# A routed expert stage with slots handed out in blocks of 64

## The reference

```python
# x: (2048, 512) after the layer norm; E = 8 experts, I = 352, top 2 of 8
logits = x @ router_w.T
probs = softmax(logits)
topk_w, topk_idx = top_k(probs, 2)
topk_w = topk_w / sum(topk_w)
for each expert e:
    acc += combine[:, e] * (silu(x @ gate_w[e]) * (x @ up_w[e]) @ down_w[e])
shared = silu(x @ s_gate_w + b) * (x @ s_up_w + b) @ s_down_w + b      # 704 wide
x = x + tanh(g_ffn[1]) * (acc + shared)
```

## Time and profile before

| | |
|---|---|
| time, median of 3 runs | 1132.05 us (1128.5 to 1133.57) |
| the profiled execution | 1127.45 us |
| its span, first to last instruction | 1125.4 us |
| busy share of the span: PE, DVE, ACT, POOL | 89%, 66%, 52%, 38% |
| granted TensorE clock over the span | 0.961 |
| stage of the tiles, PE | 845.4 us to about 1070 us, 39 tiles |

### The profile page before, as it was taken

One profiled execution on the slowest core, in us unless ns is written; L12 is line 12 of the kernel. 1 busy time (PEld: TensorE's weight loads), 2 busy tenths in 40 slices (PEclk: granted clock), 3 DMA queues, 4 the chain that ended last, 5 costly groups with the idle time before them and its releaser, 6 DMA issues. The chain is left out here.

```text
span 1125.4 us, 17282 instructions
## 1 busy us (share of the span) xinstructions
PE 1003.4 (89%) x5229; PEld 456.0 (41%) x5247; DVE 740.2 (66%) x1417; ACT 589.5 (52%) x888; POOL 430.1 (38%) x467
## 2 busy tenths in 40 slices
PE   0466879999779999999999995999999999899995
PEld 0243445555423223323332221454445555555542
DVE  6988988888788677487667858676244444433347
ACT  5897999999436677477557671524221111111110
POOL 1100435553501234133323533007508888790065
PEclk9988899999979999999999998989999999999998
DMA  8322940000532424314311032996525789865678
GB/s 322 126 75 75 303 193 1 1 1 1 130 81 75 130 63 91 96 59 82 96 35 59 22 85 82 234 358 224 220 83 115 207 209 202 198 166 128 157 286 293
DMA packets 196010, 150.88 MB, mean 134 GB/s; under 512 B 138420, under 2 KB 157492, under 8 KB 195432
## 3 DMA queue, kind: packets, MB, share of 16 engines
q1 hardware_dynamic: 187000, 121.02, 39.4%
q0 software_dynamic: 8080, 27.60, 7.3%
q10 hardware_dynamic: 864, 1.44, 0.5%
HBM read 73.03 MB, written 45.60 MB: 105 GB/s over the span
## 5 line engine op out<-in xcount | busy, mean ns | idle before, releaser
L1707 DVE CUSTOM_DVE_ANT_0 ajunk<-p_row,mask_row 128x512 bf16<-128x512 f32 x256 | 166.2, 686 | 61.1 <-PE p_row L1553 58.5
L1470 ACT ACTIVATE early_place<-p_col,mask_col,any_key 128x512 f32<-128x512 f32 x128 | 92.8, 776 | 63.2 <-PE p_col L1604 62.9
L1470 ACT ACTIVATE prob<-p_col,mask_col,any_key 128x512 f32<-128x512 f32 x128 | 93.3, 786 | 38.3 <-PE p_col L1604 37.8
L1360 POOL TENSOR_TENSOR o<-sum_a,rec 32x512 f32<-32x512 f32 x30 | 39.0, 1301 | 187.3 <-DMA rec<-inv_d 185.2
L1553 PE MATMUL p_row<-ks,early_place 99*128 99x512 f16 x256 | 100.6, 395 | 9.0 <-DVE top L1707 7.9
L1604 PE MATMUL p_col<-early_place,ks 101*128 101x512 f16 x256 | 97.7, 386 | 1.2 <-ACT early_place L1470 0.6
L2824 DVE SCALAR_TENSOR_TENSOR shid<-s_up,ssilu 128x352 f32<-128x352 f32 x39 | 20.4, 524 | 99.6 <-PE s_up L2743 99.5
L2756 PE MATMUL s_down<-mw,shT 128*128 (+1 forms) x351 | 82.1, 379 | 0.6 <-DMA shT<-shidr 0.6
L2681 ACT ACTIVATE ssilu<-s_gate 128x352 f32<-128x352 f32 x39 | 18.1, 463 | 118.4 <-PE s_gate L2743 118.4
L2743 PE MATMUL s_gate<-mw,spare 128*128 x444 | 73.8, 317 | 2.9 <-DMA spare<-x_slots 2.9
L2743 PE MATMUL s_up<-mw,spare 128*128 x444 | 72.3, 313 | 0.0
(11 more groups left out here) (380 smaller groups left out, 2132.1 us busy)
## 6 DMA issues: line engine op xcount, KB each, us to landing
x_slots<-nought SPq DMA_DIRECT2D x3, 3328.0 KB, 20.1
y_slots<-spare SPq DMA_DIRECT2D x39, 256.0 KB, 2.2
early_place<-in_ctx SPq DMA_DIRECT2D x8, 1024.0 KB, 6.2
early_place<-halves_d SPq DMA_DIRECT2D x45, 128.0 KB, 2.4
halves_d<-halves SPq DMA_DIRECT2D x18, 256.0 KB, 2.1
x<-in_x SPq DMA_DIRECT2D x4, 1024.0 KB, 7.4
w<-in_L_ffn_w SPq DMA_DIRECT2D x1, 4096.0 KB, 18.5
w<-in_L_ffn_w SPq DMA_DIRECT2D x4, 1024.0 KB, 4.7
```

The source lines that it names most:

```text
L1360: nc.gpsimd.tensor_tensor(o[q, :], (sum_a, sum_b)[g % 2][n % 2][q, :], rec[q, :], ALU.mult).then_inc(t_scaled, 1)
L1470: nc.scalar.activation(prob[s % 4][:, c, :], p_col[c][:], ACT.Exp, bias=mask_col[:, b, k:k + 1], scale=any_key[:, b:b + 1]).then_inc(t_exp, 1)
L1707: nc.vector.tensor_tensor_reduce(junk[:, n % 2, :], p_row[n % 2][:], mask_row[:, blk // HPG, :], 1.0, -3e38, ALU.add, ALU.max, top[blk % 2 ...
```

## The change

Slots are handed out in blocks of 64. TILES becomes 36 (the most that 4096 slots can need if each expert rounds up to 64, in pairs of blocks), of which FULL = 28 tiles hold one expert and the last eight hold two. The last block of expert j always lies in the second half of tile 28 + j. The remaining blocks of an expert are taken two at a time as whole tiles, in the order of the experts; single blocks left over, and whole tiles beyond 28, go to the first halves of the last eight tiles. `find_slots` and `find_owners` compute this, with more operations in the chain.

On PE the last eight tiles are written out (no loop), and each matmul in them becomes two: 64 columns of the stationary operand with the first expert's weights into partitions 0 to 63, and the other 64 columns with the second expert's weights into partitions 64 to 127. The second expert is a constant of the code, the first is read from `expert_of`. The tile count being even, the odd last tile of all engines' loops falls away, SP issues `late_T` before the last pair of tiles, and PE runs both halves of held chunk 0 between the last two down products.

```diff
-TILES = (B * S * CHOSEN + EXPERTS * (P - 1)) // P
+HALF = P // 2
+TILES = -(-((B * S * CHOSEN + EXPERTS * (HALF - 1)) // HALF) // 2)
+FULL = TILES - EXPERTS
...
-    tile_no = sb(st, "tile_no", [P, TILES, EXPERTS], F32)
+    half_no = sb(st, "half_no", [P, TILES, 2 * EXPERTS], BF16)
...
             def find_slots():
-                link(nc.vector.tensor_scalar(tiles[:], before[:, NT, :], 1.0 / P, (P - 1) / (2.0 * P), ALU.mult, ALU.add))
-                link(nc.vector.tensor_scalar(tiles[:], tiles[:], ROUND, None, ALU.add))
-                link(nc.vector.tensor_scalar(tiles[:], tiles[:], -ROUND, None, ALU.add))
-                link(nc.vector.tensor_copy(ends[:], tiles[:]))
+                link(nc.vector.tensor_scalar(singles, before[:, NT, :], 1.0 / HALF, (HALF - 1) / (2.0 * HALF), ALU.mult, ALU.add))
+                rounded(singles)
+                link(nc.vector.tensor_scalar(singles, singles, -1.0, 0.0, ALU.add, ALU.max))
+                link(nc.vector.tensor_scalar(pairs, singles, 0.5, -0.25, ALU.mult, ALU.add))
+                rounded(pairs)
+                link(nc.vector.scalar_tensor_tensor(singles, pairs, -2.0, singles, ALU.mult, ALU.add))
+                link(nc.vector.tensor_copy(ends[:], blocks[:]))
                 for e in range(1, EXPERTS):
-                    link(nc.vector.tensor_tensor(ends[:, e:e + 1], ends[:, e - 1:e], tiles[:, e:e + 1], ALU.add))
-                link(nc.vector.tensor_tensor(starts[:], ends[:], tiles[:], ALU.subtract))
-                link(nc.vector.tensor_scalar(starts[:], starts[:], float(P), None, ALU.mult))
-                link(nc.vector.tensor_tensor(before[:, 0:NT, :], before[:, 0:NT, :], starts[:].unsqueeze(1).broadcast_to([P, NT, EXPERTS]), ALU.add))
+                    link(nc.vector.tensor_tensor(ends[:, :, e:e + 1], ends[:, :, e - 1:e], blocks[:, :, e:e + 1], ALU.add))
+                link(nc.vector.tensor_tensor(starts[:], ends[:], blocks[:], ALU.subtract))
+                link(nc.vector.tensor_scalar(top, ends[:, 0, EXPERTS - 1:EXPERTS], 2.0, 2.0 * FULL, ALU.mult, ALU.max))
+                link(nc.vector.tensor_scalar(jump, pairs_end, float(FULL), None, ALU.max))
+                link(nc.vector.tensor_tensor(jump, jump, pairs_end, ALU.add))
+                link(nc.vector.tensor_tensor(jump, singles_start, jump, ALU.subtract))
+                link(nc.vector.tensor_scalar(jump, jump, top, float(P), ALU.add, ALU.mult))
+                link(nc.vector.tensor_scalar(lift, pairs_start, 2.0, -2.0 * FULL - 1, ALU.mult, ALU.add))
+                link(nc.vector.tensor_scalar(lift, lift, 0.0, float(HALF), ALU.max, ALU.mult))
+                link(nc.vector.tensor_tensor(back, number[:, 0, :], pairs_start, ALU.subtract))
+                link(nc.vector.tensor_scalar(back, back, FULL + 1.0, float(P), ALU.add, ALU.mult))
+                link(nc.vector.tensor_tensor(back, back, lift, ALU.subtract))
+                link(nc.vector.tensor_scalar(pairs, pairs, float(P), float(HALF), ALU.mult, ALU.add))
+                link(nc.vector.tensor_scalar(pairs_start, pairs_start, float(P), -float(HALF), ALU.mult, ALU.add))
+                link(nc.vector.scalar_tensor_tensor(own, count, float(HALF), each_token(back), ALU.is_lt, ALU.mult))
+                link(nc.vector.tensor_tensor(odd, count, each_token(pairs), ALU.is_ge))
+                link(nc.vector.tensor_tensor(odd, odd, each_token(jump), ALU.mult))
+                link(nc.vector.tensor_tensor(count, count, each_token(pairs_start), ALU.add))
+                link(nc.vector.tensor_scalar(shift, count, 1.0 / HALF, -(HALF - 1) / (2.0 * HALF), ALU.mult, ALU.add))
+                rounded(shift)
+                link(nc.vector.tensor_scalar(shift, shift, -2.0 * FULL, 0.0, ALU.add, ALU.max))
+                link(nc.vector.scalar_tensor_tensor(count, shift, float(HALF), count, ALU.mult, ALU.add))
+                link(nc.vector.tensor_tensor(count, count, odd, ALU.add))
+                link(nc.vector.tensor_tensor(count, count, own, ALU.add))
...
+            for n in range(2):
+                body(PAIRS_OF_TILES - 1, n, False)
...
+            def parts_of(r, n):
+                i = 2 * r + n
+                if isinstance(i, int) and i >= FULL:
+                    return ((0, HALF), expert(i)), ((HALF, P), i - FULL)
+                return (((0, P), expert(i)),)
...
-                        mm = nc.tensor.matmul(bank[n][:, 0:EI], (first_xT[:, n] if first(r) else xT[n])[:, hs, k, :], w[:, bass.ds(e * (2 * WC) + c, EI)],
-                                              start=(k == 0 and hs + hm == 0), stop=(k == KB - 1 and hs == 1))
+                        for (p0, p1), e in parts:
+                            mm = nc.tensor.matmul(bank[n][p0:p1, 0:EI], (first_xT[:, n] if first(r) else xT[n])[:, hs, k, p0:p1],
+                                                  columns(e, c, EI),
+                                                  start=(k == 0 and hs + hm == 0), stop=(k == KB - 1 and hs == 1))
...
             pe.wait_ge(e_pre, 16 * 4)
+            pe.wait_ge(e_silu, TILES - 1)
+            held_chunk(0, 0)
+            pe.wait_ge(e_hid, TILES - 1)
+            held_chunk(0, 1)
+            down(PAIRS_OF_TILES - 1, 1)
             pe.wait_ge(e_silu, TILES)
-            held_chunk(0, 0)
-            down(PAIRS_OF_TILES, 0)
+            held_chunk(1, 0)
             pe.wait_ge(e_hid, TILES)
-            held_chunk(0, 1)
-            held_chunk(1, 0)
             held_chunk(1, 1)
```

More of the change, by code:

```diff
@@ L2004, in stage_shared @@
     before = sb(st, "before", [P, NT + 1, EXPERTS], F32)
-    tiles = sb(st, "tiles", [P, EXPERTS], F32)
-    ends = sb(st, "ends", [P, EXPERTS], F32)
-    starts = sb(st, "starts", [P, EXPERTS], F32)
+    blocks = sb(st, "blocks", [P, 2, EXPERTS], F32)
+    ends = sb(st, "ends", [P, 2, EXPERTS], F32)
+    starts = sb(st, "starts", [P, 2, EXPERTS], F32)
+    jump, back, lift = (chosen[:].rearrange("p s t -> p (s t)")[:, n * EXPERTS:(n + 1) * EXPERTS] for n in range(3))
+    top = best[:, 0:1]
     slot = index8[:].bitcast(F32)
@@ L2448, in find_slots @@
-                link(nc.vector.tensor_tensor(starts[:], ends[:], tiles[:], ALU.subtract))
-                link(nc.vector.tensor_scalar(starts[:], starts[:], float(P), None, ALU.mult))
-                link(nc.vector.tensor_tensor(before[:, 0:NT, :], before[:, 0:NT, :], starts[:].unsqueeze(1).broadcast_to([P, NT, EXPERTS]), ALU.add))
+                pairs, singles, count = blocks[:, 0, :], blocks[:, 1, :], before[:, 0:NT, :]
+                pairs_end, pairs_start, singles_start = ends[:, 0, :], starts[:, 0, :], starts[:, 1, :]
@@ L2555, in all_tiles @@
                 body(r, n)
-        body(PAIRS_OF_TILES, 0)
     def first(r):
         return isinstance(r, int) and r == 0
-    def last(r):
-        return isinstance(r, int) and r == PAIRS_OF_TILES
     with nc.Block() as block:
@@ L2604, in _ @@
                     body(r, n)
-            for n in range(2):
-                body(PAIRS_OF_TILES - 1, n, n == 0)
             sp.wait_ge(m_wl, NQ * (2 + EXPERTS) + MORE)
@@ L2733, in expert, with columns, product @@
                                       skip_runtime_bounds_check_because="counts of experts, clamped to the last on chip")
-            def product(r, n, e, at, bank, done, free):
+            def columns(e, c, width, r=P):
+                return w[0:r, e * 2 * WC + c:e * 2 * WC + c + width] if isinstance(e, int) else w[0:r, bass.ds(e * (2 * WC) + c, width)]
+            def parts_of(r, n):
[3 more added lines that the diff above has]
+                return (((0, P), expert(i)),)
+            def product(r, n, parts, at, bank, done, free):
                 i = 2 * r + n
@@ L2748, in down @@
                 i = 2 * r + n
-                e = expert(i)
+                parts = parts_of(r, n)
                 pe.wait_ge(e_hT[n], 16 * (r + 1))
@@ L2755, in down @@
                         c = hm * WC + D0 + m * D
-                        mm = nc.tensor.matmul(p_down[n][:], hT[n][0:rows(m), hs, m, :], w[0:rows(m), bass.ds(e * (2 * WC) + c, D)],
-                                              start=(m == 0 and hs + hm == 0), stop=(m == EB - 1 and hs == 1))
+                        for (p0, p1), e in parts:
+                            mm = nc.tensor.matmul(p_down[n][p0:p1, :], hT[n][0:rows(m), hs, m, p0:p1], columns(e, c, D, rows(m)),
+                                                  start=(m == 0 and hs + hm == 0), stop=(m == EB - 1 and hs == 1))
                 mm.then_inc(e_down, 1)
             def body(r, n):
-                i = 2 * r + n
-                e = expert(i)
+                parts = parts_of(r, n)
                 pe.wait_ge(*((m_first[n], 16) if first(r) else (e_xin[n], 16 * r)))
-                pe.wait_ge(m_wl, NQ * e + (NQ * 3 + MORE))
-                product(r, n, e, G0, p_gate, e_gate, e_silu)
-                product(r, n, e, U0, p_up, e_up, e_hid)
+                for _, e in parts:
```

(21 more changed lines are left out.)

38 lines of the change are left out of this document (25 added, 13 removed).

## The result

The changed kernel takes 1125.37 us (median of 20 runs) beside 1131.51 us of the kernel before (20 runs in turn with it): a ratio of 0.9951, 95% interval 0.9932 to 0.997. The change makes the kernel 0.3 to 0.7% faster, just about the 0.5% that the prediction set as the bound of "no change". The time lies inside the range of 1122 to 1143 but 4.5 us under the forecast of 1129.9. It is just in the band under 1126.4, to which the prediction gave a chance of 0.25. The profiled execution of the changed kernel took 1124.75 us with a span of 1122.9, 2.7 us under the profiled execution before; the medians are 6.1 apart.

What follows compares the result with a forecast made beforehand. The prediction took PE to bound the tile stage, with POOL's gathers ending the chain: -16.6 + 3.0 + 6.2 + 1.6 + 1.0 + 2.6 = -2.2 us, median 1132.05 to 1129.9, range 1122 to 1143 (8 in 10).

Steps and rivals of the forecast that it cites:

- step 3: Before tile 25: PE waits 4.8 us for POOL's split of expert 7's weights, plus 1.4 slow clock; +6.2 us.
- Step 1: Stage of the routed tiles: three tiles fewer, 39 to 36, at 5.53 us each; -16.6 us.
- Step 2: find_slots: longer VectorE chain makes dest 6.6 us later, PE waits 2.0 before the third gate chunk; +3.0 us with clock.
- the clock, +1.0: Third gate chunk: slow matmuls after PE's 2.0 us idle stretch cost 1.0 us, bounds 0 and 1.7.
- third rival: Tile 25: no wait for expert 7, or half of it, or no clock loss; 3 to 8 us less, chance 0.22.
- clock term (1.4): Tile 25: slow clock after PE's wait for expert 7 costs 1.4 us.
- Just in time: Tile 21: expert 6 is done at 960.9, before the tile's gate starts at 963.08.
- Step 4: Eight two-expert tiles: paired half matmuls run in parallel; +1.6 us for pairs, +1.0 for four groups at 0.24 each.
- The 6 ns a pair: Two-expert tiles: each of 264 matmul pairs costs 6 ns extra; +1.6 us, bounds 0 and 19.8.
- first rival: Two-expert tiles: weight loads show in every pair, 52 ns each, 13.7 us in place of 1.6; 1142 us, chance 0.17.
- Step 5: End of the stage: two shared chunks instead of one before the last down product, so gathers start later; +2.6 us.
- straight code runs without gaps: PE's unrolled two-expert tiles: written-out code costs nothing, as the shared expert's straight code at the end runs without gaps.

Runs made afterwards that it cites:

- e4: The kernel before with 26 further linked operations in find_slots ahead of dest, results unused; one run, 1159.24 us.
- e11: The kernel before, unedited, traced again on another chip; one run, 1184.85 us.
- e10: The changed kernel with the last down product moved before the second held chunk of the shared expert; 1158.39 us, ratio 0.9894 to the kernel before.
- e9: The changed kernel with the last eight tiles as single matmuls over 128 columns, second expert of each left out; one run, 1158.48 us.
- e3: The changed kernel with all matmuls of the first half queued before all of the second in the last eight tiles; one run, 1165.95 us.
- e5: The changed kernel, unedited, on another chip; 1160.56 us, ratio 0.9948 to the kernel before.

## Why the prediction was right, and where only its sum was

The place of every step and the mechanism of the dear ones were seen right: three tiles saved, most of it paid back at tile 25. That the sum of -2.2 came so near the -2.5 of the profiles is luck: step 3 was 2.5 us too cheap, steps 1, 2 and 4 together 2.8 too dear. The way from the profile to the median failed: the prediction carried its difference over unchanged (4.6 us; 4.1 against the later median), but in the changed kernel it was 0.6. That is the missing 3.4 us, and its cause is open. They put the result into the band that the prediction called faster by over 0.5%, though the mechanism named for it, no wait for expert 7 or half of one, did not happen in the profile, where the wait was 6.79 us. In the other traces of the changed form it was 0.39 to 4.62, so in part of the executions that rival may be true.

**Step 1** held: tiles stand 5.53 us apart (two-expert ones too: 1031.17 to 1036.69), and 28 to the end of the stage is 16.1 us shorter, the 16.6 less what the pairs add.

**Step 2.** DVE, first and last operation of find_slots in the changed kernel; the earlier trace rows are their counterpart.

```profile
757.91 0.17 DVE L2460 TENSOR_SCALAR blocks<-before 128x8 f32<-128x8 f32 x1
...
768.47 0.18 DVE L2495 CAST dest<-slot_of 128x32 int32<-128x32 f32 x1
```

The chain takes 10.56 us; before it took 4.21. +6.35 for a forecast of +6.6: wide operations with a constant are 0.26 apart, not 0.33. PE's wait was 1.54 us idle for 2.0. The stage began 2.3 us later, but 0.6 of it had arisen before the chain (first gate chunk of the batch at 757.34 for 756.78), so the chain cost 1.7 us where the step had 3.0. The failed term is the clock, +1.0: no slow matmuls followed the wait, here or in e4. The length of an idle stretch does not decide it by itself: PE stood idle for 3.15 us before tile 21 in e4, and the clock granted behind it was 1.00; in e11 it stood idle for 1.99 us before the same tile, and 0.51 was granted.

**Step 3** was sized too low, 4.8 for 6.75, and is the term on which the whole turned. PE would have been at tile 25 at 988.84, 2.24 later than before, as the step said (2 and 3 cancel). It was POOL that came 1.7 us later relative to the stage, 1.4 of it a new wait for expert 5's gate weights (at 907.34). The prediction took POOL's end as fixed at 146.06; the table has it anywhere from 142.7 to 147.8. The range is that of POOL's waits for weight loads in the stage, 3.3 us in e10 and 7.0 in the first trace of the changed kernel: POOL's end less these waits is 139.4 to 140.7 in all nine traces. The prediction named these waits as a bound and as its third rival, but only for a gain. Its clock term (1.4) was 1.8: tile 25 takes 7.34 us instead of 5.53, at 0.50 of the clock. "Just in time" for expert 6 at tile 21 turned into a wait of 2.64 that cost nothing more, since tile 25 waits for POOL anyway. The same holds for a wait that no step named, 2.03 us for hidden rows at the first down product (860.59; 0.60 before).

**Step 4** was 1.8 us too dear. Per pair there is nothing: two-expert tiles inside a group are 5.52 us apart as full ones are. Per group the 0.24 is about right (5.75 where the form changes twice in a tile, and 0.8 for four groups by e9). The 6 ns a pair had no row behind them: they were a guess near the lower of two bounds, and the second pair of p_out, which showed none, was the better guide. The first rival, weight loads that show, is excluded. The weight loads themselves (count, busy us, mean ns), full and 64 columns:

```profile
L2792 PEld LDWEIGHTS s_gate<-mw,spare 128*128 128x128 f16 x312 | 31.3, 101 | 31.1 <-issue 10.8
...
L2792 PEld LDWEIGHTS s_gate<-mw,spare 128*64 128x64 f16 x192 | 10.7, 110 | 5.1 <-issue 1.3
```

A half takes as long to load as a whole (110 for 101 ns), but the loads of the two halves run side by side as well: 192 loads of 110 ns are 21.1 us and keep PEld busy for 10.7, while 312 full ones are 31.5 and keep it busy for 31.3. So a pair of half loads costs about what one full load costs, and it stays under the stream. The rule of the Trainium skill (TensorEngine Tiling (Array Packing), Restrictions) that column tiling disables Fast Weight Load may stand behind the half load that is no shorter; no run here shows whether it does, and no time is lost by it here. The same page (Key Properties) says that tiles load weights and multiply in parallel; the trace agrees in both: the loads as above, the matmuls in e3, where those of up for one half run beside those of gate for the other.

**Step 5** held: 9.28 us for 6.49, +2.8 (2.6 forecast; the rest is the changes of form). The 0.6 us more from there to the first gather stood in no term.

## What to carry to other kernels

Work that is taken off the bounding engine is worth only as much as the next engine in line allows: list, for each resource that the work needs, when it is ready, and treat that time as a range from the waits in its own chain, not as one number. A wait for a slower engine also absorbs chance delays ahead of it, so one pair of profiles can mis-size such a term by several us; compare the stretch in several traces. Two half-width matmuls cost no more than one full one if they alternate in the queue. Queued one half after the other they overlap only where one ends and the next begins: 7.1 to 7.6 us a tile here instead of 5.5.

## What the runs showed of the hardware that was not expected

On the chips of the experiments PE stands still in straight code without waiting for anything that the profile shows, in most traces before the stage (6.2 us from 800 to 830 in e5) and in all of them at the end, under the gathers. e5, PE under the gathers:

```profile
1105.27 0.38 PE L2837 MATMUL s_up<-mstg,mw 128*128 128x512 f16 x1 [1.75 <-issue]
1108.09 0.58 PE L2837 MATMUL s_up<-mstg,mw 128*128 128x512 f16 x1 [2.44 <-issue]
1110.20 0.59 PE L2837 MATMUL s_up<-mstg,mw 128*128 128x512 f16 x1 [1.53 <-issue]
```

Single matmuls between gaps of 0.3 to 2.4 us, 18.3 us in twelve gaps; on the first chip PE is busy 20.00 of the 20 us from 1080 to 1100. In e5 77.8 us lie between the first gather and the end of the span, 50.8 in the first chip's trace: with the gaps, that stretch holds 27 of the 36.7 us between the two spans (1159.6 and 1122.9). The prediction's "straight code runs without gaps" is true of the two traces of the first chip only. The cause (the fetching of instructions would fit) was not tested. The gaps did not fall on the written-out two-expert tiles in any trace looked at.
